# Second attention of a two-layer transformer: the two normalisations, the router and the sending of rows woven into its unrolled batches, stacks transposed by DMA

## What is computed

```python
h = _layernorm(x) * (1 + ca) + sa          # layer 0
x = x + ga * attention0(h)                 # normalised q and k, 16 heads of 8, gated
h = _layernorm(x) * (1 + cb) + sb
x = x + gb * experts0(h)                   # 4 experts, 1 to 4 per token
h = _layernorm(x) * (1 + ca) + sa          # layer 1: "third normalisation"
x = x + ga * attention1(h)                 # causal, 16 heads of 8
h = _layernorm(x) * (1 + cb) + sb          # "last normalisation"
x = x + gb * experts1(h)                   # 8 experts, the best 2 per token, hidden size 512
```

## Time and profile before

| | us |
|---|---|
| median of 3 runs | 2232.34 |
| lowest, highest | 2230.03, 2232.52 |
| profiled execution, time | 2230.25 |
| its span, first to last instruction | 2228.3 |
| TensorE busy | 1747.8 (78%) |
| VectorE busy | 1380.8 (62%) |
| ScalarE busy | 1190.7 (53%) |
| GpSimd busy | 898.8 (40%) |
| mean granted clock of TensorE, share of full | 0.892 |

### The profile page before, as it was taken

How to read it: one execution, slowest core, us unless ns; L and a number is a source line. 1 busy time by engine, 2 the same in 40 slices (tenths; PEclk the granted TensorE clock), 3 DMA queues, 4 the chain that set the end, 5 groups by cost and what they waited for, 6 DMA issues and landing times.

```text
span 2228.3 us, 46761 instructions
## 1 busy us (share of the span) xinstructions
PE 1747.8 (78%) x14634; PEld 956.4 (43%) x14634; DVE 1380.8 (62%) x3633; ACT 1190.7 (53%) x1780; POOL 898.8 (40%) x1789
## 2 busy tenths in 40 slices
PE   2968888888866788877999999999995440499990
PEld 2824444444435233333444444444443430277660
DVE  5445565556547777884666666666664650377766
ACT  1446767676754678752444444444445430388770
POOL 1232323232313233342434443444343477466664
PEclk9999999999975899975999999999996555699995
DMA  5099000000010000000000000000003011122227
GB/s 147 1 335 331 0 0 0 0 0 0 0 48 0 10 0 0 0 38 1 1 0 0 0 0 0 0 0 0 0 1 114 29 54 54 58 88 89 88 75 231
DMA packets 59021, 99.89 MB, mean 45 GB/s; under 512 B 8690, under 2 KB 25970, under 8 KB 57908
## 3 DMA queue, kind: packets, MB, share of 16 engines
q1 hardware_dynamic: 47216, 78.87, 10.8%
q0 software_dynamic: 9088, 18.89, 2.5%
q10 hardware_dynamic: 2628, 1.00, 0.2%
HBM read 38.84 MB, written 59.90 MB: 44 GB/s over the span
## 4 chain that ended last, share of the span: by engine, by line
PE 33%; POOL 6%; DVE 5%; issue 4%; ACT 2%; DVEq 2%; DMA 1%; POOLq 1%; ACTq 0%; SPq 0%
PE OP L1657 7%; POOL h_dram L393 5%; PE OP L1952 5%; PE SP L1937 4%; PE M L1616 4%; PE M L1572 3%; PE M L1586 2%; DVE mx L1042 2%; PE SP L1637 2%; PE M L1612 2%; PE M L1607 2%; ACT shared L637 1%; PE OP L1686 1%; PE M L1927 1%; DVE st L1001 1%
## 5 line engine op out<-in xcount | busy, mean ns | idle before, releaser
L656 ACT ACTIVATE pt<-SP 128x1024 f32<-128x1024 f32 (+1 forms) x512 | 459.7, 921 | 364.9 <-PE SP L1637 364.7
L1657 PE MATMUL OP<-pt,vs 128*32 128x256 f32 (+1 forms) x4096 | 434.4, 362 | 15.4 <-ACT pt L656 13.8
L1042 DVE TENSOR_REDUCE mx<-M 128x2 f32<-128x512 f32 (+1 forms) x384 | 257.0, 690 | 118.1 <-PE M L1616 114.9
L1657 PEld LDWEIGHTS OP<-pt,vs 128*32 128x32 f32 x4096 | 177.0, 110 | 182.6 <-issue 51.3
L475 POOL TENSOR_SCALAR_AFFINE_SELECT pt<-pt 128x256 f32<-128x256 f32 x512 | 196.0, 407 | 0.0
L403 POOL DMA_INDIRECT y_dram<-hT,dest x156 | 150.7, 966 | 108.6 <-DVE hT L1309 72.1
L751 ACT ACTIVATE pt<-SP,b 128x512 f16<-128x512 f32 x156 | 107.2, 687 | 143.0 <-PE SP L1937 116.7
L472 POOL TENSOR_TENSOR spare<-ones 128x1 f32<-128x1 f32 x256 | 49.4, 193 | 309.0 <-ACT pt L656 308.8
L1637 PE MATMUL SP<-shared,ksT 32*128 32x256 f16 (+1 forms) x2048 | 172.0, 262 | 2.4 <-ACT ksT L629 1.2
L1616 PE MATMUL M<-ksT,shared 24*128 24x128 f16 (+1 forms) x1024 | 153.5, 250 | 0.0
L442 POOL TENSOR_TENSOR ha<-hT,ones 128x256 f32<-128x256 f32 x64 | 39.6, 619 | 280.1 <-PE M L1572 270.8
(11 more groups left out here) (267 smaller groups left out, 3330.0 us busy)
## 6 DMA issues: line engine op xcount, KB each, us to landing
h_dram<-shared SPq DMA_DIRECT2D x8, 4488.0 KB, 34.3
hT<-h_dram SPq DMA_DIRECT2D x39, 264.0 KB
rows<-g_dram SPq DMA_DIRECT2D x4, 2048.0 KB, 7.1
pt<-y_dram SPq DMA_DIRECT2D x32, 256.0 KB, 3.7
x_sb<-in_x SPq DMA_DIRECT2D x8, 512.0 KB, 8.9
pt<-in_w SPq DMA_DIRECT2D x4, 1024.0 KB, 7.1
out<-x_sb SPq DMA_DIRECT2D x16, 256.0 KB, 3.0
y_dram<-hT,dest POOLq DMA_INDIRECT x156
```

What stands on the lines that cost most here:

```text
L656: act.activation(pt[:, u % 4, :, 0:W], SP[u % 2][:, :, 0:W], ACT.Exp, scale=SCALE).then_inc(s["exp"], 1)
L1042: dve.tensor_reduce(to, M[:, k % 2, :].rearrange("p (j k) -> p j k", j=2 if k < 8 else 4), AX.X, ALU.max).then_inc(s["mred"], 1)
L1657: last = pe.matmul(OP[32 * g:32 * g + 32, j // 2, c + q0:c + T], vs[:, par, k, HG * j + g, :], pt[:, u % 4, i, k * T:k * T + T - q0], star ...
```

## The change

The three phases norm(2), attention(1) and norm_rows() become one, causal(), with every batch written out (no hardware loop). Inside batch b stand: entry of batch b+3 (z by ScalarE from x_sb with a bias "away" = -mean x rstd, transpose into M, scaling into ha2), projection of batch b+2, its raw copy by ScalarE (raw), the high halves by ScalarE (high), the low halves by GpSimd (low), and four transposing DMAs on SP's queue (turn); the fills of batch b+1, the maximum and two more transposing DMAs (turn_again). The output is transposed by VectorE in 32x32 blocks from PSUM (tail_t), normalised, transposed again by VectorE (tail_n), with the rows of Wo put in the order that this gives. The last normalisation of batch b-5 or b-6 (z3, turn3, h3, router, low3, back, row, logits) stands in the same units, with statistics for four batches at a time (stats3). Choosing goes by six parts (PARTS_B) in a shorter form, and the sends of the first four parts stand between GpSimd's selects. The stack, V and the transposed k and q have two and three buffers (st2, vs3, ks3, qs3) in what was hT. The expert weights are loaded after the last values product, their split (weight_low) is VectorE's, and the table of row factors for the last combination (spread(3)) is loaded after the phase.

```diff
-QB, QN = B // NQ, NT // NQ
+PARTS_B = [(0, 8), (8, 14), (14, 20), (20, 24), (24, 28), (28, 32)]
...
+            def turn(b):
+
+                sp.wait_ge(s["lo"], b + 1)
+                if b >= 3:
+                    sp.wait_ge(s["score"], CH * (b - 2))
+                for w, dst in enumerate((qs3, ks3)):
+                    for t in range(TT):
+                        sp.dma_start(dst[b % 3][:, :, t * P:(t + 1) * P],
+                                     st2[b % 2][:, w, t * H:(t + 1) * H].rearrange("p h f d -> p (h f d)"),
+                                     transpose=True).then_inc(s[f"turned{b % 3}"], 16)
+
+            def turn_again(b):
+
+                sp.wait_ge(s["mrow"], b + 1)
+                for t in range(TT):
+                    sp.dma_start(qs3[b % 3][:, :, t * P:(t + 1) * P],
+                                 st2[b % 2][:, 0, t * H:(t + 1) * H].rearrange("p h f d -> p (h f d)"),
+                                 transpose=True).then_inc(s[f"again{b % 3}"], 16)
+
+            turn(0)
+            turn(1)
+            turn_again(0)
+            for b in range(B):
+                if b + 2 < B:
+                    turn(b + 2)
+                if b + 1 < B:
+                    turn_again(b + 1)
+            sp.wait_ge(s["pv"], CH * B)
+            weights(1)
+            phase(sp, 5)
+            spread(3)
...
+                for b in range(B):
+                    for u in range(CH):
+                        select(b, u)
+                        if u == 1 and b + 2 < B:
+                            low(b + 2)
+                            place_v(b + 2)
+                        for _ in range(2 if b == B - 1 else 1):
+                            if q < 4 and b >= PARTS_B[q][1] + 7:
+                                send(q, n)
+                                n += 1
+                                if n == 2 * TT * (PARTS_B[q][1] - PARTS_B[q][0]):
+                                    q, n = q + 1, 0
+                while q < len(PARTS_B):
+                    send(q, n)
+                    n += 1
+                    if n == 2 * TT * (PARTS_B[q][1] - PARTS_B[q][0]):
+                        q, n = q + 1, 0
...
+                def high(b):
+
+                    act.drain()
+                    if b >= 2:
+                        act.wait_ge(s[f"again{(b - 2) % 3}"], 32 * ((b - 2) // 3 + 1))
+                    heads = qkv[:, 0:2].rearrange("p w t (h d) -> p w (t h) d", d=DH)
+                    wide = [P, TT * H, 2, DH]
+                    act.activation(st2[b % 2][:, 0, :, 0:3:2, :], heads[:, 0].unsqueeze(2).to_broadcast(wide), ACT.Copy)
+                    act.activation(st2[b % 2][:, 1, :, 0:2, :], heads[:, 1].unsqueeze(2).to_broadcast(wide),
+                                   ACT.Copy).then_inc(s["hi"], 1)
...
+                for b in range(B):
+                    exp(b, 0)
+                    if b + 2 < B:
+                        raw(b + 2)
+                        high(b + 2)
+                    if b - 1 in CHOSEN:
+                        route_exp(CHOSEN.index(b - 1))
+                    for u in range(1, 5):
+                        exp(b, u)
+                    if b + 3 < B:
+                        z2(b + 3)
+                    if b >= 5:
+                        z3(b - 5)
+                    exp(b, 5)
+                    exp(b, 6)
+                    if b >= 6:
+                        row(b - 6)
+                    exp(b, 7)
+                    if b + 3 < B:
+                        enter(b + 3)
+                    if b >= 5:
+                        h3(b - 5)
...
+                def tail_t(b, i):
+
+                    dve.wait_ge(s["pv"], CH * b + 4 * i + 4)
+                    dve.transpose(oT[:, 2 * i:2 * i + 2, :].rearrange("p j t -> p (j t)"), OP[:, i, :]).then_inc(s["o"], 1)
+
+                def tail_n(b):
+
+                    dve.drain()
+                    o = oT[:].rearrange("p j (s c) -> p j s c", c=32)
+                    v = rs[:].rearrange("p (j s) o -> p j s o", j=NJ)
+                    dve.reciprocal(v, o[:, :, :, DH:DH + 1])
+                    dve.drain()
+                    dve.tensor_tensor(an[:].rearrange("p (s j) d -> p j s d", j=NJ), o[:, :, :, 0:DH],
+                                      v.to_broadcast([P, NJ, T // 32, DH]), ALU.mult)
+                    dve.drain()
+                    dve.transpose(aT[:], an[:].rearrange("p n d -> p (n d)")).then_inc(s["aT"], 1)
...
+                FILLS = [0, 3, 3, 3, 3, 0, 0, 0]
...
+                for b in range(B):
+                    done = 0
+                    for u in range(CH):
+                        score(b, u)
+                        if CH * b + u >= 2:
+                            values((CH * b + u - 2) // CH, (u - 2) % CH)
+                        if u == 0 and b + 2 < B:
+                            project(b + 2, 0)
+                            project(b + 2, 1)
+                        if u == 4 and b:
+                            tail_wo(b - 1)
+                        for k in range(done, done + FILLS[u]):
+                            if b + 1 < B:
+                                fill(b + 1, k)
+                        done += FILLS[u]
+                        if u == 5 and b >= 6:
+                            router(b - 6)
+                            back(b - 6)
+                        if u == 6:
+                            if b + 3 < B:
+                                enter(b + 3)
+                            if b >= 5:
+                                turn3(b - 5)
+                        if u == 7 and b - 1 in CHOSEN:
+                            positions(CHOSEN.index(b - 1))
+                values(B - 1, CH - 2)
+                values(B - 1, CH - 1)
+                tail_wo(B - 1)
+                for n in range(B - 5, B + 1):
+                    if n < B:
+                        turn3(n)
+                    router(n - 1)
+                    back(n - 1)
+                    if n == B - 3:
+                        positions(4)
+                positions(5)
```

More of the change, by code:

```diff
@@ L36 @@
 NEG = -1e30
+LOWEST = -3e38
 MSHIFT = 256.0
@@ L153, in program @@
         rstd = sb("rstd", [P, NT])
+        away = sb("away", [P, NT])
         dev = sb("dev", [P, NT])
@@ new lines, in causal @@
+                for b in range(B):
+                    if b >= 6:
+                        low3(b - 6)
+                    for k in range(12):
+                        if b + 1 < B:
+                            fill_max(b + 1, k)
+                        if b and k == 0:
+                            tail_t(b - 1, 1)
+                        if b and k == 2:
+                            tail_n(b - 1)
+                        if b and k == 8:
+                            tail_x(b - 1)
+                    if b + 1 < B:
+                        max_row(b + 1)
+                    if b:
+                        tail_stats(b - 1)
+                    tail_t(b, 0)
+                    if b >= 6:
+                        logits(b - 6)
+                    if b >= 4 and b % 4 == 0:
+                        stats3(b // 4 - 1)
+                    if b in CHOSEN:
+                        choose(CHOSEN.index(b))
+                    if b - 1 in CHOSEN:
+                        place(CHOSEN.index(b - 1))
@@ new lines, in causal @@
+                low3(B - 6)
+                tail_t(B - 1, 1)
+                tail_n(B - 1)
+                tail_x(B - 1)
+                tail_stats(B - 1)
+                stats3(7)
+                logits(B - 6)
+                for n in range(B - 5, B):
+                    low3(n)
+                    logits(n)
+                    if n == B - 5:
+                        choose(4)
+                    else:
+                        weight_low(n - (B - 4))
+                    if n == B - 4:
+                        place(4)
@@ L1895, in norm_rows @@
-                positions(NQ - 1)
+                                                hh[:, n % 2, v, t * P:(t + 1) * P], ident16[:])
+                    last.then_inc(s["back"], 1)
+                FILLS = [0, 3, 3, 3, 3, 0, 0, 0]
+                enter(0)
+                enter(1)
+                for b in range(2):
+                    for t in range(TT):
+                        project(b, t)
+                for k in range(12):
+                    fill(0, k)
+                enter(2)
+                for b in range(B):
+                    done = 0
[9 more added lines that the diff above has]
+                        for k in range(done, done + FILLS[u]):
+                            if b + 1 < B:
+                                fill(b + 1, k)
[10 more added lines that the diff above has]
+                            positions(CHOSEN.index(b - 1))
```

656 lines of the change are left out of this document (440 added, 216 removed).

## The result

| | before | after |
|---|---|---|
| median, us | 2231.19 (4 runs, 2229.67 to 2232.52) | 2264.72 (4 runs, 2251.68 to 2265.44) |
| ratio, 95% interval | | 1.0137 (1.0099 to 1.0174) |
| profiled execution, time / span | 2230.25 / 2228.3 | 2264.46 / 2262.8 |
| mean granted clock | 0.892 | 0.817 |

The account below looks back on a forecast made before the run. TensorE's own list of work was taken to set the batch period, with time to gain outside the batches. First score 1012, plus batches 97.5 + 535.6 + 9 + 26, tail 79, blocks 304.9: span 2064, time 2066 us; range 2005 to 2180.

Parts of the forecast that it names:

- TensorE in a batch: TensorE's work per batch: transposes removed, router and other products added, net -1.35 us, a floor of 19.0 us.
- VectorE in a batch: Fills in units 1 to 4: VectorE sets 11.6 us; with TensorE's 8.3 and 0.7 of waits, 20.6 us a batch.
- a clock under 0.9 in the batches: Listed sign that the forecast is wrong: TensorE's granted clock in the batches below 0.9.
- Lead-in: Ahead of the first score: third normalisation goes, 38 us instead of 62.5, first score at 1012, 24 us gained.
- Period: Time of one steady batch: 20.6 us, for 26 batches from 5 to 30, 535.6 us.
- Transposing DMAs: Six per batch on SP's queue, 1.2 us each, near a plain copy; the second pair fits with 0.6 us to spare.
- Last batch: Final batch without fills, two sends per unit between GpSimd's selects: 26 us to its end.
- Tail: From batches' end to first expert block: weight loads, split, choosing, placing, sixteen sends, rows table; 79 us, first block at 1759.
- A: Rival: SP's queue of transposing DMAs is the period, 31 us and more a batch, time about 2390; chance 0.12.
- B: Rival: only the second pair of transposing DMAs lands 1 to 2 us late, period 22, time 2110; chance 0.2.
- C: Rival: VectorE overlaps better and TensorE's floor holds, period 19.3, time 2032; chance 0.12.
- D: Rival: GpSimd's sends delay selects, +1 us in ten batches, and the tail is 20 longer; time 2096; chance 0.1.

Follow-up runs that it names:

- e7: e1 without the 16 sends of part 3 between the last batch's selects, which go out behind that batch; median 2084.61 us.
- e8: e7 with two 256-column products ahead of fills 2, 5, 8 and 10, eight ahead of fill 2 in batches with a placing; median 2063.55 us.
- e1: Changed kernel with VectorE's reciprocal, multiply and transpose of the output dealt out behind maxima 2, 4 and 6; median 2097.04 us.
- e2: Kernel before, with the maximum of fill 4 taken four times over in each batch; 2446.79 us.
- e4: Changed kernel with 7 products of 256 columns ahead of fill 5 of each batch from the second on; 2175.13 us.
- e6: e1 with TensorE's counting products for the placing of rows moved from unit 7 to unit 6, ahead of the next entry; median 2089.30 us.

## Why the prediction was wrong

**The step that failed** is in "TensorE in a batch" and "VectorE in a batch": the floor of 19.0 and the period 11.6 + 8.3 + 0.7 = 20.6 us were worked out with durations of the earlier trace rows, all taken at clock 1.00, and nothing in the sum asked whether the new list would keep that clock (it stands only among the signs of being wrong, "a clock under 0.9 in the batches", without a price). That VectorE would set this stretch was seen, 11.6 us long; in the sum its lead stood as spread ("small waits"), though tail_n in one piece gives a wait of 1.76 us. The term for that piece was too small as well: "the normalising of the output 1.25" is about the length of the two pieces before, and tail_n takes 1.75 (1419.50 to 1421.25), with a multiply of 0.80 and a transpose of its own, 0.45, that the sum leaves out. Measured in place of 20.6 us: 27.3 us, of which 17.0 at half clock. 31 x 6.7 = 208 us, where the whole miss is 2264.5 - 2066 = 198; some of the first batches were shorter.

Everything else of the sum can be read against a version where the clock holds. In the traces (e7 and e8 also lack the last batch's sends):

| | predicted | changed | e1 | e7 | e8 |
|---|---|---|---|---|---|
| first score, us | 1012 | 1016.8 | 1016.8 | 1015.9 | 1015.0 |
| batch from 7 on, no sends or placing | 20.6 | 27.3 | 20.0 | 20.0 | 20.0 |
| last values end | 1680 | 1879.4 | 1709.7 | 1680.3 | 1671.6 |
| first block | 1759 | 1958.7 | 1789.0 | 1759.0 | 1749.8 |
| time (profiled) | 2066 | 2264.5 | 2094.9 | 2064.3 | 2055.0 |

- *Lead-in*: 19.5 us gained, 24 forecast. Most of the miss lies ahead of the first fill, at 1000.45, 26.8 us in for a forecast of 22, where TensorE waits 7.24 us for the first DMAs (6 forecast). The first score waited 4.37 us for the second pair, which with the row shift I gave 4.
- *VectorE's stretch*: the transpose of 128x512 from PSUM took 0.70 to 0.72 (priced 0.69), the multiply 0.80 in one piece beside GpSimd, 0.42 behind maximum 4.
- *Period*: 20.0 for 20.6 in an ordinary batch; at full clock a batch with sends takes 20.3 to 20.6, one with a placing 21.2 to 21.5 (e7). The split of the floor doesn't add up: 19.0 less 10.4 leaves 8.6, where the sum has 8.3. *Early batches*: 20.0 for 19.5 in e1, with TensorE waiting 1.5 us for the second pair in each of the batches 0 to 3, 2.9 in batch 4. So the 4.3 us of cover were too much here, where unit 5 has no router products yet; from batch 6 on most of these waits are gone or under 1 us.
- *Transposing DMAs*: 1.23 to 1.27 us for 1.2, 2.5 to landing. In the earlier trace rows a plain DMA of 128 KB comes to an estimated 2.2 us to landing, between 1.5 and 3.0. The Trainium skill (VectorE: DVE Perf Modes, The three transpose paths) has 1309 ns for 128x128; here 128x512 take that long. What the Trainium skill says in Advanced Engine Details and Errata, X-Bar Transpose, that they "are as fast as regular DMAs", fits better.
- *Last batch*: 26 forecast, 26.6 in the changed kernel (first select 1852.82, last values' end 1879.4). Without sends between its selects it takes 12.8 (e7) at no cost behind it, so it was their place in GpSimd's list that put them on the path.
- *Tail*: 79.3 for 79. But its terms erred both ways: the placing of part 5 ends at 1923.8, +44.4 for +47.5, and the sends of part 4 ran slower (single ones up to 3 us, beside VectorE's splitting) and ended at +47 for +44, so that 32 sends in a row, 1901.64 to 1948.45, set the end.
- *Blocks*: 304.1 for 304.9.

**The rivals.** A (the queue is the period) fell with 1.27 us a DMA. B's late pair shows mainly in the early batches, and its 1.4 us a batch hold no price for a lower clock; of the period's 27.3 us the clock takes 7.3. C: the ordinary batches of e1 and e8, 20.0, lie between the forecast's 20.6 and C's 19.3. D: at full clock a batch with sends takes 0.3 to 0.6 us longer (e7), about half of D's 1 us; at half clock nothing shows (27.3 to 27.4), and in the last batch it is more. No rival of the prediction had the right end; the slower side was given only to A. That the forecast of 2066 is met by e8 (2063.6) is in part luck: e8 has another last batch and products in the waits, its shorter period offsets its longer lead-in, and its median holds single falls of the clock that the forecast didn't count.

Why I held the fall for unlikely: the forecast has TensorE busy over 0.9 of a batch, and the earlier trace rows show 0.94 at full clock. The share over a batch was the wrong quantity. From 1100 us on e7 has 0.90 at mean clock 0.96, the changed kernel 0.91 at 0.68, since at half clock it never waits; in its 10.2 us at full clock it is busy for 0.80. The profile before could have warned: from 1011.3 to 1036.2 TensorE is busy 0.81 of a stretch that runs at 0.50 throughout.

## What to carry to other kernels

When a change lengthens the work of another engine between two releases, work out how long TensorE will stand still **in one place**, not only what the period becomes; 1.76 us of standing still cost 7.3 us a batch here. Deal side work out in pieces no longer than the slack of the double buffer, and check the granted clock inside one period (by windows of 2 us in the profile) as well as over a stage. If a wait can't be removed, useless products into a bank that is overwritten later are cheaper than the clock.

## What the runs showed that was not expected

- **The clock locks to the batch.** In the changed kernel, in e2 (another work list, other lines) and in part of the batches of e4 the period is the same 27.3 us, though split 10.2 + 17.0 in one and 13.7 + 13.6 in the other. At half clock TensorE is busy without a gap for 17.0 or 13.6 us; then full clock is back, TensorE reaches the wait, and the clock falls again. The Trainium skill describes such a cycle (TensorE: Matmul & The Clock Gate, HAM oscillation — how this bites in real kernels) for a kernel that waits 3 to 5 us for a transfer, and another for short, frequent gaps between groups of matmuls (A second HAM failure mode: psum-queue depth-cycling). The traces agree with the second: waits of 0.87 to 1.76 us, once a batch, were enough.
- **The clock isn't decided by the kernel alone.** e1, e7, e8 and e9 scatter by 15 to 37 us from run to run, e6 by 4, before by 5, and where they scatter a longer time goes with a lower mean clock. Near the edge a measurement of one run tells little: the profiled executions of e1 and e7 differ by 30 us, their medians by 12.
- **VectorE's multiply with two SBUF operands takes 0.80 us beside GpSimd's tensor operations and 0.43 alone**; the maxima that read PSUM take 0.69 beside them too. The Trainium skill (GPSIMD Engine Reference, Specifications) names the shared SBUF interfaces and contention "with two SBUF inputs"; the trace agrees.
